# ScalarE weights gathered rows in the ranking half of layer 0, and two node counts change place, in a four-layer graph network kernel

## The reference

```python
i, j = (g[0], g[1])                       # sources, destinations
weighted_info = x[i] * ew[:, None]
aggr_out = jax.ops.segment_sum(weighted_info, j, num_segments=x.shape[0])
...
x = _layernorm(x + aggr_out, axis=-1)
```

## Time and profile before

| | us |
|---|---|
| median of 3 runs | 10578.48 |
| lowest, highest | 10572.45, 10578.76 |
| the profiled execution | 10576.3 |
| its span, first to last instruction | 10574.5 |

### The profile page before, as it was taken

One profiled execution on the slowest core, in us unless ns is written; L12 is line 12 of the kernel. 1 busy time (PEld: TensorE's weight loads), 2 busy tenths in 40 slices (PEclk: granted clock), 3 DMA queues, 4 the chain that ended last, 5 costly groups with the idle time before them and its releaser, 6 DMA issues. The chain is left out here.

```text
span 10574.5 us, 94116 instructions
## 1 busy us (share of the span) xinstructions
PE 2992.5 (28%) x20557; PEld 2564.7 (24%) x20557; DVE 6908.4 (65%) x9464; ACT 4574.6 (43%) x5711; POOL 6596.9 (62%) x6626
## 2 busy tenths in 40 slices
PE   1212766774000000000002366666665500000002
PEld 1111666774000000000002344454444300000002
DVE  7888777776221212227996488888888577777775
ACT  1111544553111211115773277777776144444442
POOL 6777756664677777770002477777775177777774
PEclk9999767776555555555555666666676655555555
DMA  3343422221332332324552344444443277777773
GB/s 107 94 97 86 87 82 58 72 69 45 82 113 99 117 113 101 114 105 174 203 207 93 69 137 136 136 136 135 133 131 112 71 241 236 236 237 237 236 236 110
DMA packets 722785, 1395.95 MB, mean 132 GB/s; under 512 B 409551, under 2 KB 439452, under 8 KB 715094
## 3 DMA queue, kind: packets, MB, share of 16 engines
q0 software_dynamic: 287072, 587.19, 21.0%
q1 hardware_dynamic: 406642, 636.11, 18.2%
q10 hardware_dynamic: 28996, 171.86, 4.5%
HBM read 827.48 MB, written 602.51 MB: 135 GB/s over the span
## 5 line engine op out<-in xcount | busy, mean ns | idle before, releaser
L808 POOL DMA_INDIRECT l_rows<-in_x,l_idx x1568 | 1678.1, 1070 | 789.0 <-issue 442.0
L2426 POOL DMA_INDIRECT l_rows<-table,l_idx x1568 | 1483.3, 946 | 685.4 <-issue 472.4
L1906 POOL DMA_INDIRECT l_rows<-h,l_idx x1568 | 1542.0, 983 | 589.1 <-issue 423.2
L1288 POOL DMA_INDIRECT rows<-l_rows,l_idx x1568 | 1501.2, 957 | 524.9 <-issue 496.9
L1941 PE MATMUL l_made<-l_kv_w,l_rows_t 128*128 128x256 f32 x3136 | 1088.3, 504 | 775.3 <-ACT l_kv L1971 472.8
L2502 ACT ACTIVATE l_lifted<-l_rows,l_up 128x256 f32<-128x256 f32 x1568 | 639.5, 460 | 1020.4 <-DMA l_rows<-table,l_idx 1020.4
L1941 PEld LDWEIGHTS l_made<-l_kv_w,l_rows_t 128*128 128x128 f32 x3136 | 756.2, 258 | 986.1 <-issue 855.8
L1679 PE MATMUL l_wide<-l_diag,l_ones 128*128 128x384 f32 x4 | 3.3, 927 | 3127.0 <-DVEq L1709 3127.0
L1277 DVE TENSOR_TENSOR l_rows<-l_run,l_weights_ps 128x56 f32<-128x56 f32 x56 | 12.0, 215 | 1320.0 <-POOLq L88 1319.8
L1248 ACT COPY l_rows<-l_run 128x1792 f32<-128x1792 f32 x56 | 190.7, 3405 | 1557.6 <-POOLq L88 1548.7
L1679 PEld LDWEIGHTS l_wide<-l_diag,l_ones 128*128 128x128 f32 x4 | 1.0, 310 | 3127.9 <-DVEq L1709 3127.9
(11 more groups left out here) (384 smaller groups left out, 12863.2 us busy)
## 6 DMA issues: line engine op xcount, KB each, us to landing
sums<-l1s_out ACTq DMA_DIRECT2D x56, 1988.0 KB, 6.8
sums<-l_out SPq DMA_DIRECT2D x112, 924.0 KB, 4.4
spread<-zeros SPq DMA_DIRECT2D x28, 3612.0 KB, 13.0
l_spread<-spread SPq DMA_DIRECT2D x112, 903.0 KB
l1s_rows<-rows SPq DMA_DIRECT2D x56, 1008.0 KB, 5.7
spread<-zeros SPq DMA_DIRECT2D x56, 938.0 KB
l_spread<-spread SPq DMA_DIRECT2D x56, 938.0 KB, 13.8
sums<-l_out ACTq DMA_DIRECT2D x56, 896.0 KB, 3.7
```

Source lines behind the costliest of these rows:

```text
L808: pool.indirect_dma_start(rows[:, b, t], None, a["x"], bass.IndirectOffsetOnAxis(ap=idx[:, b, t:t + 1], axis=0)) \
L1288: pool.indirect_dma_start(g["rows1_d"], bass.IndirectOffsetOnAxis(ap=idx[:, b, t:t + 1], axis=0), rows[:, b, t], None).then_inc(sent[b], 16)
L1906: pool.indirect_dma_start(rows[:, c.r, t, 0:C], None, g["h2_d"], bass.IndirectOffsetOnAxis(ap=idx[:, c.r, t:t + 1], axis=0)).then_inc(got[ ...
L2426: pool.indirect_dma_start(rows[:, b, t], None, g["table3_d"], bass.IndirectOffsetOnAxis(ap=idx[:, b, t:t + 1], axis=0)) \
```

## The change

In the ranking half DVE's `weigh` is gone. ACT copies the chunk's 28 weights to `share` at step r = 0 of the turn, waits at r = 1 for the gathered rows of this chunk, and in each of the steps r = 1 to 7 makes four instructions, each multiplying one column of 128 x 64 by its weight per partition and writing it with a stride into `data`, which now has two buffers. It signals `rows_used` with the last, and after a drain `weighed`, for which DVE waits ahead of the scan.

The count for dst moves to the histogram half: it stands in the src part, behind the second pass of the loop, that is after 4 of the 14 src chunks. ACT issues the read of its row right after writing the dst positions, and waits for that write before it. The count for src moves to layer 1's first pass, between chunks 28 and 29; SP reads its row there, behind the first chunk's load and ahead of the second's. The gather of `head_a`, which needs it, moves from the block before to the end of that pass on POOL. Two semaphores of the normalisations become one set, and the integer scratch `part` shares the storage of `pos_i`.

```diff
-    PARTS = (0, turns // 8), (turns // 8, turns // 4), (turns // 4, turns // 2)
+    PARTS = ((0, turns // 4),), ((0, 2), (2, turns // 4))
...
-            data = s.sb("l0_data", [P, C, T + 1])
+            data = s.sb("l0_data", [P, 2, C, T + 1])
+            share = s.sb("l0_share", [P, 2, T])
...
-                        with v.Fori(0, turns // 4) as h:
-                            for b in range(2):
-                                ranking.hist_vector(v, n, h * 4 + b * 2)
-                                ranking.hist_vector(v, n, h * 4 + (b * 2 + 1))
-                                weigh_early(h + turns // 4 * n, b)
-                                sum_rows(h + turns // 4 * n, b, data_ps)
+                        for part, (begin, end) in enumerate(PARTS[n]):
+                            if part == 1:
+                                v.wait_ge(ends_in, 16)
+                                partition_nodes(v, g, "dst", ends)
+                            with v.Fori(begin, end) as h:
+                                for b in range(2):
+                                    ranking.hist_vector(v, n, h * 4 + b * 2)
+                                    ranking.hist_vector(v, n, h * 4 + (b * 2 + 1))
+                                    weigh_early(h + turns // 4 * n, b)
+                                    sum_rows(h + turns // 4 * n, b, data_ps)
...
-                    for n, (begin, end) in enumerate(PARTS):
-                        with v.Fori(begin, end) as h:
-                            for b in range(2):
-                                for r in range(TURN):
-                                    ranking.vector_step(v, h * 2 + b, r)
-                                weigh(h + turns // 2, b)
-                                sum_rows(h + turns // 2, b, data)
-                        if n < len(KEYS):
-                            v.wait_ge(ends_in, 16 * (n + 1))
-                            counts.partition_nodes(v, g, KEYS[n], ends_row, scratch_row).then_inc(ends_read, 1)
+                    with v.Fori(0, turns // 2) as h:
+                        for b in range(2):
+                            for r in range(TURN):
+                                ranking.vector_step(v, h * 2 + b, r)
+                            wait(v, weighed[b], h + 1)
+                            sum_rows(h + turns // 2, b, data[:, b])
...
                         write_first(n)
+                        if n == 0:
+                            act.wait_ge(first_out, 32)
+                            act.dma_start(ends.row[:], g["first_d"]["dst"][1:NP + 1].rearrange("n o -> o n").to_broadcast([P, NP])).then_inc(ends_in, 16)
...
                         for r in range(TURN):
                             ranking.scalar_step(nc, act, h * 2 + b, r)
+                            if r == 0:
+                                nc.scalar.copy(share[:, b], weight[:, bass.ds(((h + turns // 2) * 2 + b) * T, T)])
+                            else:
+                                if r == 1:
+                                    act.drain()
+                                    wait(act, got[b], (h + (turns // 2 + 1)) * (16 * T))
+                                for t in range((r - 1) * 4, r * 4):
+                                    last = nc.scalar.mul(data[:, b, :, t + 1], rows[:, b, t], share[:, b, t:t + 1])
                             if r == 3:
                                 if before:
                                     store(*before)
                                 keeps(h + turns // 2, b)
+                        last.then_inc(rows_used[b], 1)
+                        act.drain().then_inc(weighed[b], 1)
...
                     load(0, 0)
+                    sp.dma_start(ends.row[:], g["first_d"]["src"][1:NP + 1].rearrange("n o -> o n").to_broadcast([P, NP])).then_inc(ends_in, 16)
                     with sp.Fori(0, NC // 2 - 1) as h:
...
+                    for n, (begin, end) in enumerate(((0, NC // 4), (NC // 4, NC // 2))):
+                        if n == 1:
+                            v.wait_ge(ends_in, 16)
+                            partition_nodes(v, g, "src", ends).then_inc(counted, 1)
...
+                    pool.wait_ge(counted, 1)
+                    pool.indirect_dma_start(head_a[:], None, g["tablea_d"],
+                                            bass.IndirectOffsetOnAxis(ap=g["head_key"]["src"][:], axis=0)).then_inc(head_in, 16)
```

More of the change, by code:

```diff
@@ L233, in first_positions @@
         v.drain()
[L235 to L261, removed]
 def split_keys(v, key, part, low, high):
@@ L300, in __init__ @@
         self.low, self.high = s.sb(f"{name}_low", [P, L + 3 * SB], BF16), s.sb(f"{name}_high", [P, L + 3 * SB], BF16)
[L301 removed]
+        self.key = s.sb(f"{name}_key", [P, L], I32)
         self.hot_low = s.sb(f"{name}_hot_low", [P, HOT, SB, P], BF16)
@@ L714, in scalar, with __init__, partition_nodes @@
         nc.scalar.activation(stat[:, 2], stat[:, 1], ACT.Sqrt).then_inc(self.rooted, 1)
+class Ends:
+    def __init__(self, s, name):
+        self.row, self.scratch = s.sb(f"{name}_ends_row", [P, NP]), s.sb(f"{name}_scratch_row", [P, NP // 2], BF16)
+        self.edge, self.ended = s.sb(f"{name}_edge", [P, 4]), s.sb(f"{name}_ended", [P, 2, 4])
+def partition_nodes(v, g, k, ends):
+    for n, past in enumerate((-float(L), -1.0, 0.0, float(L))):
+        v.tensor_scalar(ends.edge[:, n:n + 1], g["run_end"][:], past, None, ALU.add)
+    v.drain()
+    half = NP // 2
+    for part in range(2):
+        for n in range(4):
+            v.tensor_scalar(ends.scratch[:], ends.row[:, part * half:(part + 1) * half], ends.edge[:, n:n + 1], 0.0,
+                            ALU.is_le, ALU.add, accum_out=ends.ended[:, part, n:n + 1])
+            v.drain()
+    v.tensor_tensor(ends.ended[:, 0], ends.ended[:, 0], ends.ended[:, 1], ALU.add)
+    v.drain()
+    head, tail, through, after = (ends.ended[:, 0, n:n + 1] for n in range(4))
+    v.tensor_copy(g["head_key"][k][:], head)
+    v.tensor_copy(g["tail_key"][k][:], tail)
+    v.tensor_tensor(through, through, tail, ALU.is_gt)
+    v.tensor_tensor(after, after, tail, ALU.is_gt)
+    v.drain()
+    v.tensor_scalar(through, through, -OFF, None, ALU.mult)
+    v.tensor_scalar(after, after, OFF, -OFF, ALU.mult, ALU.add)
+    v.drain()
+    v.tensor_tensor(g["cross_key"][k][:], tail, through, ALU.add)
+    v.drain()
+    v.tensor_tensor(g["last_key"][k][:], g["cross_key"][k][:], after, ALU.add)
+    return v.drain()
 def layer0(nc, a, sem, g):
@@ L952, in _ @@
                     turn(0, 1, (turns // 2, 0))
-                    read_ends(0)
-                    for n, (begin, end) in enumerate(((1, turns // 8 + 1), (turns // 8 + 1, turns // 2))):
-                        if n == 1:
-                            act.wait_ge(ends_read, 1)
-                            read_ends(1)
-                        with act.Fori(begin, end) as h:
-                            turn(h, 0, (h + (turns // 2 - 1), 1))
-                            turn(h, 1, (h + turns // 2, 0))
+                    with act.Fori(1, turns // 2) as h:
+                        turn(h, 0, (h + (turns // 2 - 1), 1))
+                        turn(h, 1, (h + turns // 2, 0))
                     store(turns - 1, 1)
+                    act.wait_ge(first_out, 32 * len(KEYS))
                     for b in range(2):
```

74 lines of the change are left out of this document (32 added, 42 removed).

## The result

The changed kernel takes 10422.13 us (median of 4 runs, 10418.78 to 10425.13) against 10578.62 of the kernel before (4 runs). The ratio is 0.9855 with a 95% interval of 0.9842 to 0.9868: 156 us faster. The forecast was 10487, 91 us faster, in a range of 10390 to 10555.

What follows compares the result with a forecast made beforehand. Ranking half bound by DVE's work plus waits in the ring of DVE, PE and ACT; histogram half and layer 1's first pass by POOL. -64 + 5 - 65 + 29 + 4 = -91 us gave 10487 us, range 10390 to 10555.

Steps and rivals of the forecast that it cites:

- What bounds the stage: Ranking half: no engine full; DVE's own 39.7 us plus 9.3 us of waits make a 49.0 us turn.
- The price of a multiplication: ACT in the ranking half: 0.24 us per 128x64 multiplication (bounds 0.14 and 0.40), 6.7 us a turn.
- The longest wait of the turn grows by 1.0 us: Ranking half, r = 3: four multiplications join ACT's store, flags and next mask, adding 1.0 us (0.6 to 1.6).
- Net gain of a turn: 2.2 to 2.3: Ranking half: 3.2 us leave DVE, 1.0 us returns through ACT; 28 turns give -64 us.
- rival 1: Ranking half: PE's shorter idle gap raises its clock near 1; turns of 41 to 43 us, total 10365, chance 0.18.
- The rule that multiplications belong on VectorE: Ranking half: by this rule alone a turn would lose 3.4 us and the stage 95; the forecast went against it.
- The counts: Leaving the ranking half gives -65 us; dst costs +29 in the histogram half, src 0 in layer 1.
- The first turn: Ranking half's start: its gather starts only after the histogram half and takes 36 us; +5 us (0 to 10).
- Layer 1's start: Layer 1's first pass: the src count's row, queued ahead, may delay the first scatter; +4 us (0 to 12).
- Rival 3: Ranking half: gathered rows arrive too late for ACT, turns of 52.7 us, total 10655, chance 0.05.
- the 9 to 10 called free: Ranking half: gathered rows may arrive up to 9 or 10 us after a turn's end at no cost.
- Rivals 2 and 4: 2: ranking turns no shorter, PE sets longer steps, 10551, chance 0.15; 4: counts not hidden, layer 1 delayed, 10525, chance 0.07.

Runs made afterwards that it cites:

- e9: Changed kernel plus one unused DVE product of about 3.1 us behind step 7 of each turn; 10580.57 us against 10580.84 of the kernel before, ratio 1.000.
- e10: Changed kernel with ACT's flags and store at step r = 1, ahead of the gather wait, not r = 3; 10332.62 us against 10580.84 of the kernel before.

## Why the prediction was right, and where its size was off

* **What bounds the stage: right.** DVE's own work plus waits in the ring; what was taken from DVE at the turn's end came off there (e9 puts 3.18 us back, the end grows by 2.9).
* **The price of a multiplication: right.** 0.24 us estimated, 0.24 measured, 0.97 for four.
* **"The longest wait of the turn grows by 1.0 us": right for ACT's row, partly luck for the step.** ACT's row at r = 3 grew by 0.94 us. The step's mean went from 8.55 to 9.45, but because the turns with 6.35 and 8.3 to 8.9 went; those of 9.3 to 9.8 came to 9.3 to 9.5. The 49.0 us of a turn, from which the sum started, was a mean over such unlike turns as well.
* **"Net gain of a turn: 2.2 to 2.3": this is the step that failed.** It measured 49.0 - 44.36 = 4.6. The sum put the clock's effect at nothing and left it to rival 1. Of the 4.6, some 3 is DVE's work gone, -0.9 the longer mean of the long step, and 2.5 the steps around it, 1.9 of them the two behind it, where PE no longer works at the lower clock. e9 shows the last part by reversing it. That the total still fell inside the range is owed to the half of rival 1 that the range took in. Rival 1 foresaw the mechanism and asked for a turn of 41 to 43 us; it came half way, the granted clock rising from 0.71 to 0.80 and not near 1. The gap of 8.57 us had become 5.28; the second, behind ACT's block, had grown from 3.67 to 4.51 us and still brought the clock down to 0.50 in every turn, for 6.8 us. Why the low stretch is never longer with the change stays open. The Trainium skill, page "TensorE: Matmul & The Clock Gate", Part 1, has activity keep the clock up and idleness drop it; e9 agrees, with steps of 6.36 us and 0.71 as the gap went back to 8.2.
* **The rule that multiplications belong on VectorE** (the Trainium skill, page "ScalarE: Activation LUTs", Rules for kernel authors) would have made the stage 95 us longer at the rows' prices. It measured the other way, 126 us shorter in 27 turns with the counts taken off, the part of the clock included: ACT's busy share rose, and its 6.7 us a turn lay mostly beside its waits.
* **The counts: right.** -65 is consistent with the -191 of the turns (65 + 27 x 4.6 = 189). For dst +29 was forecast, the count itself cost 30.4, and 3.3 more came at the change of key. The prediction had "a few us" there for ACT's flags, if their cover failed; the cover held, and it was the gather behind the row of positions that came later, which the sum didn't have. For src 0, measured 1.5 at its chunk and nothing in the sum.
* **The first turn: mis-sized.** +5 forecast, +8.9 measured, inside 0 to 10. Layer 1's start: +4 forecast, measured none.
* **Rival 3, rows too late: did not occur,** though rows that came 9.3 us behind the turn's end, of the 9 to 10 called free, show how close the point was. In e10 it began to show at step 3.
* **Rivals 2 and 4** are out: turns did get shorter, and the counts were hidden where they should be.

## What to carry to other kernels

When work leaves an engine of a ring, add up not only what goes from its path: look at what the others do with the shorter gap. Before taking a mean turn, list the turns: if steps of one kind come in two lengths and the granted clock lies between its levels, the mean hides a part that can go or come back as a whole. Here it was worth about as much as the path's own gain, and one small instruction put back took both away. And an engine that waits for data at a known place should do its block work there: moving 5.8 us of copies from a full place to an idle one gave 90 us, more than half of what the whole change had given, by moving two calls.

## What the runs showed of the hardware

* The same kernel took 10579 and 10581 us in two series and 11757 to 11964 on three other chips, with waits named remote on DVE, ACT and POOL. On one of those the change gave a ratio of 0.9905 instead of 0.9855, and moving the store nothing more that can be told. So the gain in this ring depended on the chip.
* An indirect DMA's issue on POOL took 4.59 us beside a DVE scan of 4.02, mostly 0.94 otherwise. Beside the counts (compare with accumulation) it was not lengthened: POOL was busy 1501.2 us in layer 1's pass before and 1501.6 after, with one count in it.
* A gather whose last issue was made on time landed 3.3 us later while a row of 3136 KB was on its way.
* Steps behind the long one last 6.36 us where the granted clock is 0.50, and 3.97 where it is 1.00 and DVE sets the pace. Turns of the kernel before with gaps of PE equal to 0.02 us have the clock low for 6.8 us or for 23.9.
